# Gated FFN with quantised down projection: down products one batch later, one weight tile kept, loads for batch 2 issued in batch 0

## The reference

```python
scale = cond @ norm_w.T + 1.0
ms = jnp.mean(x * x, axis=-1, keepdims=True)
h = x * (scale[:, None, :] * jax.lax.rsqrt(ms + EPS))
u = h @ up_w.T
val, gate = jnp.split(u, 2, axis=-1)
h = val * jax.nn.gelu(gate, approximate=False)
hq = h + jax.lax.stop_gradient(act_quant(h) - h)       # round(h * 127/max|h| of the row), clipped, scaled back
wq = down_w + jax.lax.stop_gradient(weight_quant(down_w) - down_w)   # round(w / mean|w|) to -1, 0, 1
y = hq @ wq.T
return y + x
```

## Time and profile before

| | |
|---|---|
| median of 3 runs | 813.84 us (813.39 to 815.17) |
| the profiled execution | 815.42 us, of which span 813.6 us |
| PE busy | 773.3 us (95%) |
| PE weight loads | 637.2 us (78%) |
| DVE busy | 603.5 us (74%) |
| ACT busy | 444.0 us (55%) |
| POOL busy | 252.9 us (31%) |
| mean granted TensorE clock | 0.981 of 2.4 GHz |
| DMA | 130.88 MB, mean 161 GB/s |

### The profile page before, as it was taken

The page is one execution under the profiler, slowest core; times in us unless marked ns, Lnnn a source line. Parts: engine busy times, 40 slices in busy tenths (PEclk is TensorE's granted clock), DMA queues, the critical chain, the costliest instruction groups (busy, mean ns, idle before and its releaser), DMA issues.

```text
span 813.6 us, 17562 instructions
## 1 busy us (share of the span) xinstructions
PE 773.3 (95%) x6401; PEld 637.2 (78%) x6401; DVE 603.5 (74%) x855; ACT 444.0 (55%) x1023; POOL 252.9 (31%) x314
## 2 busy tenths in 40 slices
PE   5898989899899999999999999999999999999987
PEld 4687878778668897789868887789778987888853
DVE  5897987869456895489756995489647995589577
ACT  5687767477533654355535655366535654455523
POOL 3876965357211232123211223123211232111100
PEclk9799999999899999999999999999999999999999
DMA  6435763836445154535455255525645345515512
GB/s 217 158 124 182 251 215 129 318 106 222 153 182 195 56 194 147 186 118 176 169 172 180 90 180 168 183 75 184 202 129 180 113 157 187 188 46 187 185 52 78
DMA packets 34507, 130.88 MB, mean 161 GB/s; under 512 B 3224, under 2 KB 3744, under 8 KB 34464
## 3 DMA queue, kind: packets, MB, share of 16 engines
q1 hardware_dynamic: 33920, 130.04, 47.1%
q10 hardware_dynamic: 544, 0.27, 0.1%
HBM read 110.89 MB, written 19.40 MB: 160 GB/s over the span
## 4 chain that ended last, share of the span: by engine, by line
PE 71%; DVE 6%; DMA 2%; ACT 1%; issue 1%; SPq 0%; DVEq 0%; ACTq 0%
PE A L1062 11%; PE A L1065 11%; PE A L1064 11%; PE Y L1114 11%; PE B L1065 8%; PE B L1062 8%; PE B L1064 8%; DVE h L843 2%; DMA xin<-in_x_dram 2%; PE X L1010 1%; DVE mpart L822 1%; DMA w_scratch<-wslots 1%; DVE h L809 1%; PE X L1102 1%; DVE q L848 1%
## 5 line engine op out<-in xcount | busy, mean ns | idle before, releaser
L1062 PE MATMUL A<-xT,wslots 128*128 (+1 forms) x1024 | 281.3, 275 | 15.5 <-ACT snapC L599 12.2
L1065 PE MATMUL A<-xT,wslots 128*128 (+1 forms) x1024 | 281.5, 275 | 0.0
L1064 PE MATMUL A<-xT,wslots 128*128 (+1 forms) x1024 | 281.4, 275 | 0.0
L496 POOL TENSOR_TENSOR snapC<-snapC 128x256 f32<-128x256 f32 x128 | 101.9, 796 | 494.6 <-ACT snapC L599 494.2
L1062 PE MATMUL B<-xT,wslots 128*128 (+1 forms) x768 | 210.7, 274 | 0.7 <-DVE h L803 0.7
L1064 PE MATMUL B<-xT,wslots 128*128 (+1 forms) x768 | 210.7, 274 | 0.0
L1065 PE MATMUL B<-xT,wslots 128*128 (+1 forms) x768 | 210.6, 274 | 0.0
L809 DVE SCALAR_TENSOR_TENSOR h<-h,c_all,g 128x512 f32<-128x512 f32 (+1 forms) x128 | 106.6, 833 | 127.0 <-ACT g L622 126.3
L1062 PEld LDWEIGHTS A<-xT,wslots 128*128 128x128 f16 x1024 | 100.8, 98 | 32.2 <-ACT snapC L599 14.1
L1064 PEld LDWEIGHTS A<-xT,wslots 128*128 128x128 f16 x1024 | 100.9, 99 | 14.7
L1065 PEld LDWEIGHTS A<-xT,wslots 128*128 128x128 f16 x1024 | 101.0, 99 | 12.4
(11 more groups left out here) (136 smaller groups left out, 936.9 us busy)
## 6 DMA issues: line engine op xcount, KB each, us to landing
wslots<-w_scratch SPq DMA_DIRECT2D x84, 896.0 KB, 4.7
w_scratch<-wslots SPq DMA_DIRECT2D x12, 896.0 KB, 4.6
wst<-in_L_cond_up_w_dram SPq DMA_DIRECT2D x16, 512.0 KB, 5.7
xin<-in_x_dram SPq DMA_DIRECT2D x8, 1024.0 KB, 7.3
dwb<-in_L_cond_down_w_dram SPq DMA_DIRECT2D x16, 512.0 KB, 4.6
wst<-in_x_dram SPq DMA_DIRECT2D x28, 256.0 KB, 5.5
out_dram<-wst SPq DMA_DIRECT2D x28, 256.0 KB, 5.1
xin<-in_x_dram SPq DMA_DIRECT2D x4, 256.0 KB, 4.0
```

The source lines that it names most:

```text
L496: pool.tensor_tensor(snapC[:, s % 2, 0:H], snapC[:, s % 2, 0:H], snapC[:, s % 2, H:T], ALU.add)\
L1062: pe.matmul(into, high, xh, start=(start and kp == 0), stop=False, skip_group_check=not start)
L1064: pe.matmul(into, high, xl, start=False, stop=False, skip_group_check=not start)
L1065: mm = pe.matmul(into, low, xh, start=False, stop=last, skip_group_check=not start)
```

## The change

- Down products of batch b - 2 run in batch b (before: of batch b - 1), in the same steps 10, 12, 13, 14. Batch 1 has none, and the last batch has those of batch 5. q and dq have two halves, chosen by b % 2; DOWN_AFTER_1 goes.
- KEPT is 1: tile 0 stays, tiles 1 to 15 go through the four slots of the ring. Batch 0 stores 15 tiles, each later batch loads 15.
- The loads of slots 4, 1 and 2 and of x for batch 1's step and batch 2 are issued by SP while batch 0 runs: load_slot(1, 4) before the store of tile 15, then load_slot(1, 1), the second down piece, load_x(2), load_slot(1, 2). Load_slot(1, 3) opens batch 1. The third down piece and later ones are loaded between slot loads.
- The down pieces are clipped in steps 0, 2, 3, 5, 6, 9, 11, 13 of batch 1 (before: 0, 1, 2, 4, 5, 7, 8, 9).
- In the tail ACT scales the banks of batch 6 (y_scale) and POOL adds the residual; DVE rounds five of the eight pairs of the last batch, ACT three (before: four and four), and the clip follows the rounding, on f16 (before: ahead of it, on f32).

```diff
-    KEPT = 4
+    KEPT = 1
-    LOADS = (FT - KEPT) // RING
+    LOADS = [len(range(r, FT - KEPT, RING)) for r in range(RING)]
-    STAGED_AT = {0: 0, 1: 1, 3: 2, 5: 3}
+    ROUNDED_ON_ACT = [1, 3, 5]
-    DW_CLIP = {s: i for i, s in enumerate((0, 1, 2, 4, 5, 7, 8, 9))}
+    DW_CLIP = {s: i for i, s in enumerate((0, 2, 3, 5, 6, 9, 11, 13))}
-    DOWN_AFTER_1 = {12: 0, 13: 1, 14: 2, 15: 3}
+    DW_LOAD_WITH = {6: 3, 7: 4, 9: 5, 10: 6, 13: 7}
-        q = sb("q", [P, FT * T], F16)
+        q = sb("q", [P, 2 * FT * T], F16)
+        def q_tiles(b, s, n):
+            return q[:, bass.ds(b % 2 * (FT * T) + s * T, n * T)]
...
             def load_slot(b, s):
-                sp.wait_ge(gate_psum, FT * b + (s - RING + 1 if s >= KEPT + RING else s - RING + 1 - KEPT))
+                r = ring_of(s)
+                held = s - RING if s >= KEPT + RING else KEPT + r + RING * (LOADS[r] - 1) - FT
+                sp.wait_ge(gate_psum, FT * b + (held + 1))
...
             def batch(b, first=False, final=False):
-                load_slot(b, 7)
-                if not final:
+                load_slot(b, 3)
+                if not final and not first:
                     sp.wait_ge(xT_psum, KT * b + KT)
                     load_x(b + 1)
...
+                for s in range(5, 15):
                     load_slot(b, s)
+                    if first and s in DW_LOAD_WITH:
+                        load_dw(DW_LOAD_WITH[s], PIECES + DW_LOAD_WITH[s])
                 if not first:
+                    store_y(b - 2, 0)
+                    load_xres(b - 2, 2)
+                load_slot(b, 15)
+                if not final:
+                    load_slot(b + 1, 4)
+                if not first:
+                    store_y(b - 2, 1)
+                    load_xres(b - 2, 3)
+                    store_y(b - 2, 2)
+                if not final:
+                    load_slot(b + 1, 1)
+                else:
+                    load_xres(BEFORE, 0)
+                if not first:
+                    store_y(b - 2, 3)
+                if not final:
+                    load_slot(b + 1, 2)
+                else:
+                    load_xres(BEFORE, 1)
...
+                if s == FT - 2:
+                    load_dw(0, PIECES)
+                    sp.wait_ge(w_stored[ring_of(4)], 16 * LOADS[ring_of(4)])
+                    load_slot(1, 4)
+            for s in (1, 2):
+                sp.wait_ge(w_stored[ring_of(s)], 16 * LOADS[ring_of(s)])
                 load_slot(1, s)
+                if s == 1:
+                    load_dw(1, PIECES + 1)
+                    sp.wait_ge(xT_psum, 2 * KT)
+                    load_x(2)
+            sp.wait_ge(w_stored[ring_of(3)], 16 * LOADS[ring_of(3)])
             batch(1, first=True)
...
             gate_second(LAST, FT - 1)
+            for t in range(TT):
+                pool.wait_ge(yb_scaled, t + 1)
+                pool.wait_ge(xres_loaded[t % 2], 32 * BEFORE + 16 * (t // 2 + 1))
+                pool.tensor_tensor(ystage[:, t % 2, :], ystage[:, t % 2, :], xres[:, t % 2, :], ALU.add).then_inc(yb_done, 1)
...
+            def y_scale(t):
+                act.wait_ge(dq_ready, BEFORE + 1)
+                act.wait_ge(y_psum, TT * BEFORE + (t + 1))
+                act.wait_ge(ystage_free[t % 2], 32 * BEFORE + 16 * (t // 2 + 1))
+                act.activation(ystage[:, t % 2, :], Y[t % 2][:, :], ACT.Copy, scale=dq_of(BEFORE, t)).then_inc(yb_scaled, 1)
...
-            for i in range(1, PAIRS, 2):
+            y_scale(0)
+            y_scale(1)
+            for i in ROUNDED_ON_ACT:
                 add_magic(i)
                 q_round(i)
+                if i == ROUNDED_ON_ACT[0]:
+                    y_scale(2)
+                    y_scale(3)
...
-                    if not final and s - 1 in down_after:
-                        staged_out(b - 1, down_after[s - 1])
+                    if not first and s - 1 in DOWN_AFTER:
+                        staged_out(b - 2, DOWN_AFTER[s - 1])
...
+            for i in range(PAIRS):
+                q_scale(LAST, i)
+                if i not in ROUNDED_ON_ACT:
+                    qe_round(i)
+                if i >= 2:
+                    qe_clip(i - 2)
+            for i in range(PAIRS - 2, PAIRS):
+                qe_clip(i)
...
-                    if not final and s in down_after:
-                        if first and down_after[s] == 0:
-                            pe.wait_ge(dT_ready, PIECES)
-                        down_tile(b - 1, down_after[s])
+                    if not first and s in DOWN_AFTER:
+                        down_tile(b - 2, DOWN_AFTER[s])
...
             batch(1, first=True)
+            pe.wait_ge(dT_ready, PIECES)
             with pe.Fori(2, LAST) as b:
```

More of the change, by code:

```diff
@@ L384, in batch @@
                     load_dw(2, PIECES + 2)
[L385 to L397, removed]
-                    load_slot(b, s)
[L399 to L405, removed]
-                if not first:
[L407 to L412, removed]
-                load_slot(b + 1, 6)
-                store_y(b - 1, 3)
+                else:
+                    load_xres(b - 2, 0)
+                    load_xres(b - 2, 1)
+                for s in range(5, 15):
+                    load_slot(b, s)
+                    if first and s in DW_LOAD_WITH:
+                        load_dw(DW_LOAD_WITH[s], PIECES + DW_LOAD_WITH[s])
+                if not first:
+                    store_y(b - 2, 0)
[15 more added lines that the diff above has]
+                    load_slot(b + 1, 2)
+                else:
+                    load_xres(BEFORE, 1)
             for t in range(TT):
@@ L443, in _ @@
             for t in range(TT):
-                store_y(BEFORE, t)
+                sp.wait_ge(yb_done, t + 1)
+                sp.dma_start(out_v[BEFORE, :, t, :], ystage[:, t % 2, :]).then_inc(ystage_free[t % 2], 16)
                 if t + 2 < TT:
@@ L853, in q_clip, with qe_round @@
                 dve.tensor_scalar(q_of(b, i), q_of(b, i), QMAX, QMIN, ALU.min, ALU.max).then_inc(q_ready, 1)
+            def qe_round(i):
+                dve.wait_ge(q_scaled, PAIRS * LAST + (i + 1))
+                dve.tensor_scalar(q_of(LAST, i), h_tiles(LAST, 2 * PAIR_ORDER[i], 2), MAGIC, MAGIC, ALU.add, ALU.subtract)\
+                   .then_inc(qe_rounded, 1)
             def qe_clip(i):
[L856 to L863 removed]
+                if i in ROUNDED_ON_ACT:
+                    dve.wait_ge(qe_rounded_act, ROUNDED_ON_ACT.index(i) + 1)
+                else:
+                    dve.wait_ge(qe_rounded, i + 1 - sum(j < i for j in ROUNDED_ON_ACT))
+                dve.tensor_scalar(q_of(LAST, i), q_of(LAST, i), QMAX, QMIN, ALU.min, ALU.max).then_inc(qe_ready, 1)
             def y_out(b, t, bank, res, stage):
@@ L867, in y_out @@
                 dve.wait_ge(y_psum, TT * b + (t + 1))
-                dve.scalar_tensor_tensor(out=stage, in0=bank[:, :], scalar=dq_of(b)[:, t:t + 1], in1=res,
+                dve.scalar_tensor_tensor(out=stage, in0=bank[:, :], scalar=dq_of(b, t), in1=res,
                                          op0=ALU.mult, op1=ALU.add).then_inc(y_done, 1)
@@ L904, in batch @@
                         q_clip(b - 1, s - QUANT_FROM)
-                    down_after = DOWN_AFTER_1 if first else DOWN_AFTER
-                    if not final and s - 1 in down_after:
-                        staged_out(b - 1, down_after[s - 1])
+                    if not first and s - 1 in DOWN_AFTER:
+                        staged_out(b - 2, DOWN_AFTER[s - 1])
                     of, before = (b, s - 1) if s else (b - 1, FT - 1)
@@ L985, in _ @@
             quant_scale(LAST)
-            for i in range(PAIRS + 1):
-                if i < PAIRS:
-                    q_scale(LAST, i)
-                if i in STAGED_AT:
-                    staged_out(BEFORE, STAGED_AT[i])
-                if i < PAIRS:
-                    qe_clip(i)
-                if i > 0 and i % 2:
-                    qe_round(i - 1)
+            for i in range(PAIRS):
[6 more added lines that the diff above has]
+                qe_clip(i)
             dve.wait_ge(x_loaded, 16 * B)
@@ L1111, in down @@
             def down(b, t, bank, steps, first, last):
-                of = q_end if is_final(b) else q
                 for s in steps:
-                    mm = pe.matmul(bank[:, :], of[:, s * T + t * P:s * T + (t + 1) * P], dT[:, s, :],
+                    mm = pe.matmul(bank[:, :], q_tiles(b, s, 1)[:, t * P:(t + 1) * P], dT[:, s, :],
                                    start=(s == first), stop=(s == last))
@@ L1121, in down_tile @@
                     pe.wait_ge(q_ready, PAIRS * b + PAIRS)
-                    if t >= 2:
+                    if isinstance(b, int) and b == BEFORE:
+                        if t >= 2:
+                            pe.wait_ge(yb_scaled, t - 1)
+                        else:
+                            pe.wait_ge(y_done, TT * b + (t - 1))
+                    elif t >= 2:
```

(5 more changed lines are left out.)

62 lines of the change are left out of this document (25 added, 37 removed).

## The result

The changed kernel takes 809.61 us (median of 6 runs, 808.25 to 811.18), beside 813.62 us for the kernel before in the same comparison (812.5 to 815.17). The ratio is 0.9949, with an interval of 0.9932 to 0.9967: faster by 0.5%, where 1.6% was forecast. The sign is right; the size is outside the range of 796 to 808. Its profiled execution took 809.22 us, with a span of 807.4 us against the 800.9 forecast. One of the four executions of the kernel with all four edits, further down, took 1150.15 us at a mean granted clock of 0.66; its ratio leaves that one out.

What follows compares the result with a forecast made beforehand. PE was taken to bound all but batch 1 and the tail. Span: 813.6 - 22.8 (batch 1) + 13.8 (last batch) - 4.0 (tail) + 0.3 (batch 0) = 800.9 us; median 801.1, range 796 to 808.

Steps and rivals of the forecast that it cites:

- First stall: Batch 1: ACT's squares of x(2) wait 3.69 us for their load; with load_x(2) issued earlier, that wait goes.
- Slot 2: Batch 1: slot 2's load lands at 153.9, wanted at 153.2; 0.5 us taken for this and ACT's lateness together.
- Second stall: Batch 1, step 10: x_out(2) waits for DVE's x_low(1); the stall stays, with 3.4 us left at PE.
- Batch 0: Three more stores stand before weight loads in SP's queue; load_w(7) is tightest; 0.3 us taken, bounds 0 and 2.
- That is free: Loop: 15 slot loads instead of 12 per batch, at a DMA share of 0.48, cost nothing.
- rival (d): Loop: PE computes q's run-time address for 320 down products; fully exposed 14.7 to 32 us, 816 to 833; chance 0.06.
- Tail: After the last batch: PE's waits of 2.07 and 1.76 us go; 4.0 us gained, with 1.0 us of cover.
- From the span to the median: Whole kernel: span 800.9 plus 1.8, less the old profiled run's 1.6 above its median, gives 801.1 us.
- (b): Late loads of slots 1 and 2 or batch 0's weights stall PE 2 to 3 us: 804 to 807; chance 0.17.
- (a): Batch 1's second stall shrinks, with no contention and no clock loss at PE: 797 us; chance 0.13.
- (c): POOL's additions or a late y_scale break the tail's cover, up to 4 us back: 802 to 805; chance 0.07.
- (e): Batch 1 finds another limit, ACT's dT work in steps 11 to 15, and loses the gain: 812 to 815; chance 0.04.

Runs made afterwards that it cites:

- all four edits: Changed kernel with batch 0's weight loads earlier, slot 2 loaded before x(2), batch 1's later x work one step later, q_scale a step ahead: 796.83 us.
- thin clips: Changed kernel with POOL's two clip operations on 8 of 1024 columns and ACT's rounding without its constant, down weights not quantised: 807.10 us.

## Why the prediction was right or wrong, point by point

**What bounds the kernel: right.** Batch 1 and the tail were the only stages with room, and the two places gave what was gained.

**First stall: right.** The x wait went, as the sum had it.

**Slot 2: the term was mis-sized.** The rate was 3.6 us per MB and not 3.34, and the queue started 2.0 us later, because batch 0 was late. The wait for slot 2 came to 1.7 us where 0.5 stood for it and ACT together: 1.2 us. My own working had the slot 0.7 us late, and I reasoned that down by a rate without latency that no row showed.

**Second stall: right mechanism, mis-sized by a microsecond, and its due time was never questioned.** From the maxima of batch 1 to the end of x_low(1) I had 201.3 - 149.66 = 51.6 us; it was 206.78 - 151.65 = 55.1. Of the 3.5 us more, 1.3 lie ahead of step 4, nearly all of it the slot wait, and 2.2 lie on DVE behind the start of step 4 (40.2 us for 36.0 + 2.0), where contention has 2.7 by the thin clips and I had 2.0. The other 1.5 of DVE's lateness against the steady batch were there without the clips as well and are not resolved further. From x_low(1) to the waiting product it was 0.2 us longer. The stretch behind the stall was 31.6 us and not 32.9, since less of it ran at half clock (granted 0.85 over the first 10 us, 0.72 in the kernel before); that gave 1.3 back, by luck as far as the runs show. Sum: 2.4 us.

**Batch 0: mis-sized, and by the largest factor.** I had 0.3 us, with a bound of 2.0, and it was 2.0 (149.66 to 151.65). The tightest load was the one I had named: w_scale(7) starts 1.4 us late (56.30 for 54.88), while w_scale(6) is not late at all (49.36 for 49.37). I had queued load_w(7) as from 48.2, with the rate of another stretch. Its own store stands before it and waits for the tile's last part, so it was issued at 49.29 and not at 48.55; and from the down piece, issued at 48.14, to its landing 8.1 us passed for 1.96 MB, for the 6.5 that I had. The rest is not from this load: the delay falls to 0.9 us at w_scale(13) (106.52 for 105.61) and is back at 1.6 at w_scale(14) (113.35 for 111.79), since DVE waits 1.10 us ahead of it for ACT's w_high, where it was 0.45; and 0.27 us is PE's wait for slot 1.

**"That is free" in the loop: wrong.** The traffic is free, as said (90.0 us with the new ring and the old addresses). But rival (d) had the right mechanism, register operations for q's address, and the wrong engine. I looked for it on PE, where 64 of them cost nothing. It costs on DVE, eight a pass, where a dependent pair of instructions has one between them. The working listed the new addresses on PE's side only; q_round writes q too. 0.45 x 5 = 2.2 us. A steady batch over 90.1 us and a PE wait for a slot load in step 2 were two of the signs that I had named for being wrong; both came.

**Tail: right.** 114.7 us against 114.4. The timeline of PE shows its only idle time, and POOL's shows an addition that the margin was about:

```profile
798.72 1.04 PE L1142 MATMUL A<-dT,q 128*128 128x512 f16 x4 [0.29 <-DVE q L895]
```

```profile
789.07 1.27 POOL L564 TENSOR_TENSOR wst<-wst 128x512 f32<-128x512 f32 x1 [4.51 <-ACT wst L662]
```

```profile
789.47 1.15 DVE L895 TENSOR_SCALAR q<-q 128x1024 f16<-128x1024 f16 x1
```

One clip, beside that addition, took 1.15 us instead of 0.42, and one rounding, beside the addition at 783.28, 0.94 instead of 0.69. That POOL and DVE contend, as the GPSIMD Engine Reference of the Trainium skill (Specifications) says, agrees with these rows. It hit one of the four clips that I had priced, and the 1.0 us of margin held it.

**From the span to the median: wrong by 2.0 us.** I took the old profiled run's 1.6 us above its median as something that the new kernel would share. Its profiled run was 0.4 us below its own median. The distance of a profiled run from the median belongs to that run, and is no term of a kernel.

**The rivals.** What came is (b), late loads, in both places that it named: 1.7 + 1.2 = 2.9 us, just under the low end of its 3 to 6. I gave it 0.17 and took it for an alternative to the forecast, when it could add to other misses. (d) came on another engine, at 2.2 us for the 14.7 to 32 that it was priced at. (a), (c) and (e) did not come. Each miss alone stays within the range: 1.7, 2.4, 2.2, 0.3 and 2.0 us, all of one sign, make the 8.5 with rounding, and the range had 7 above the forecast.

## What to carry to other kernels

When an operand's address becomes one that is worked out at run time, look on every engine that reads or writes it for a pair of instructions in which the second waits for the first: there the register operation carries the wait, and its time and the start behind it are exposed. Issue the first of the pair a step ahead and it costs nothing. When a transfer is put ahead of others in one queue, price also the wait that it carries, since all that stands behind it in the queue waits too, and take the rate from the same stretch of the kernel. And where a stall is to remain, ask whether its work has to be due there at all: moving the due times by a step was worth more (4.8 us) than the speed-up of the late work that was tried (2.5 us with thin clips).

## What the runs showed of the hardware that was not expected

- A register operation of 57 ns between two dependent DVE instructions costs 0.12 us from start to start (1.24 to 1.36), and 64 of 46 ns on PE, between products of 379 ns, cost nothing (a pass of 90.05 us with them and without).
- Beside two tensor_scalar operations of POOL (1.29 and 1.08 us) DVE's four f32 normalisations of 512 columns took 3.68 us instead of 1.67, and beside the next one (1.57 us) an f32 rounding took 1.20 instead of 0.69 and an f16 clip 1.25 instead of 0.43. With POOL's operations cut to 8 columns it was 2.04, 0.69 and 0.43.
- Stalls of PE of the same length (4.41, 4.42 and 4.42 us, in three kernels) were followed by stretches of 31.6, 32.8 and 32.6 us with the same work, at a granted clock of 0.83, 0.66 and 0.66 over 10 us around the stall's end. A stall is thus not priced by its length alone.
- One stall of PE, 5.52 us at the jump back from the first to the second pass of the loop of one kernel, has no releaser in the profile. Only this kernel loads instructions in its second pass (5 transfers, in all others none). Its cause stays open.
